# First head's operands moved inside SBUF; second batch's transposes, rotation sums and the bias matmuls placed in the first heads

## What is computed

```
xn = layernorm(x)
# branch A: causal attention, 16 heads of 8 dims, rotary positions
q, k, v = split(xn @ qkv_w.T + qkv_b);  q = rope(q);  k = rope(k)
A = softmax(causal(q @ k.T / sqrt(8))) @ v;  A = A @ out_w.T + out_b
# branch B: six nodes, each an attention of 8 heads of 16 dims over earlier nodes
for c in range(6):
    q = ew[c,0] * (nodes[in_q] @ We[eq] + be[eq]);  k, v likewise
    nodes[c] = act_w[c] * mha(q, k, v, Wq[c], Wk[c], Wv[c], Wo[c]) + q
B = layernorm(nodes[5]) * ln_g + ln_b
return x + A + B
```

## Time and profile before

| | us |
|---|---|
| median of 3 runs (lowest, highest) | 1428.02 (1425.81, 1428.82) |
| profiled execution, device time | 1432.52 |
| profiled execution, span | 1430.7 |
| TensorE busy in the span | 1388.9 (97%) |
| VectorE busy | 1256.0 (88%) |
| ScalarE busy | 1137.6 (80%) |
| GpSimd busy | 447.0 (31%) |
| mean granted TensorE clock, as a share of full speed | 0.986 |

### The profile page before, as it was taken

One profiled execution on the slowest core, in us unless ns is written; L12 is line 12 of the kernel. 1 busy time (PEld: TensorE's weight loads), 2 busy tenths in 40 slices (PEclk: granted clock), 3 DMA queues, 4 the chain that ended last, 5 costly groups with the idle time before them and its releaser, 6 DMA issues.

```text
span 1430.7 us, 60748 instructions
## 1 busy us (share of the span) xinstructions
PE 1388.9 (97%) x26482; PEld 931.6 (65%) x26482; DVE 1256.0 (88%) x1557; ACT 1137.6 (80%) x2127; POOL 447.0 (31%) x932
## 2 busy tenths in 40 slices
PE   6899999999999999999999999999999999999996
PEld 5467777656667566676676665766667666667662
DVE  8788999898989889899898898998989989989784
ACT  3378888688878878888788788887888878878793
POOL 5331114334322332233323332234223432330110
PEclk9899999999999999999999999999999999999997
DMA  8131112344232332333323223333233332321212
GB/s 251 36 126 50 59 51 95 118 130 140 71 122 83 122 106 69 100 105 101 107 80 125 99 76 100 106 114 107 75 100 106 97 109 78 127 97 56 64 40 64
DMA packets 115940, 138.22 MB, mean 97 GB/s; under 512 B 14954, under 2 KB 90347, under 8 KB 115547
## 3 DMA queue, kind: packets, MB, share of 16 engines
q1 hardware_dynamic: 115675, 134.33, 29.0%
HBM read 64.90 MB, written 62.26 MB: 89 GB/s over the span
## 4 chain that ended last, share of the span: by engine, by line
PE 84%; DMA 5%; SPq 4%; DVE 3%; ACT 2%; POOL 2%; issue 1%; ACTq 0%; POOLq 0%; DVEq 0%
PE s L992 51%; PE cps L1087 24%; PE misc L992 8%; DMA qs<-mrows 3%; SPq L419 1%; ACT probs L761 1%; DMA dram_raw_b<-csb 1%; DVE neg_max L942 1%; PE misc L987 1%; SPq L387 1%; SPq L456 1%; DMA ks<-dram_qk_a 0%; DMA ks<-dram_qk_b 0%; POOL parts L585 0%; POOL xtok L644 0%
## 5 line engine op out<-in xcount | busy, mean ns | idle before, releaser
L761 ACT ACTIVATE probs<-s 128x512 f32<-128x512 f32 x1792 | 1059.2, 599 | 227.7 <-PE s L992 166.0
L942 DVE TENSOR_REDUCE neg_max<-s 128x1 f32<-128x1024 f32 x768 | 936.2, 1222 | 71.2 <-PE s L992 16.4
L992 PE MATMUL s<-qs,ks 99*32 99x512 bf16 (+2 forms) x7680 | 808.4, 371 | 8.6 <-DMA qs<-mrows 6.7
L992 PE MATMUL s<-ks,qs 96*32 96x512 bf16 (+2 forms) x7680 | 606.7, 370 | 6.3 <-DMA ks<-dram_qk_a 4.1
L1087 PE MATMUL cps<-probs,vs 128*32 128x256 f32 (+1 forms) x7552 | 590.8, 368 | 0.3 <-ACT probs L761 0.3
L992 PEld LDWEIGHTS s<-qs,ks 99*32 99x32 bf16 x7680 | 235.6, 94 | 245.2 <-ACT probs L761 101.4
L1087 PEld LDWEIGHTS cps<-probs,vs 128*32 128x32 f32 x7552 | 314.4, 110 | 77.5 <-issue 17.1
L992 PEld LDWEIGHTS s<-ks,qs 96*32 96x32 bf16 x7680 | 290.4, 97 | 90.5 <-issue 24.7
L617 POOL TENSOR_TENSOR mparts<-neg_max,zeros 128x8 bf16<-128x8 f32 x128 | 25.8, 201 | 788.7 <-DVE neg_max L942 657.1
L938 DVE CUSTOM_DVE_ANT_0 s<-s,mask_q 128x1024 f32<-128x1024 f32 (+7 forms) x256 | 188.2, 786 | 27.5 <-PE s L992 17.8
L683 POOL TENSOR_TENSOR parts<-full,zeros 128x512 bf16<-128x512 f32 x48 | 61.5, 1282 | 52.8 <-DVE full L918 52.8
(11 more groups left out here) (128 smaller groups left out, 603.2 us busy)
## 6 DMA issues: line engine op xcount, KB each, us to landing
dram_qk_b<-parts SPq DMA_DIRECT2D x48, 384.0 KB, 3.3
qs<-dram_qk_b SPq DMA_DIRECT2D x96, 192.0 KB
ks<-dram_qk_b SPq DMA_DIRECT2D x96, 192.0 KB
dram_qk_b<-parts SPq DMA_DIRECT2D x48, 256.0 KB, 3.2
dram_raw_b<-csb SPq DMA_DIRECT2D x95, 128.0 KB, 4.4
dram_qk_b<-parts SPq DMA_DIRECT2D x48, 128.0 KB, 3.2
vsrc<-srcT SPq DMA_DIRECT2D x12, 512.0 KB, 3.2
ctx_b<-dram_raw_b SPq DMA_DIRECT2D x44, 128.0 KB
```

The lines of the kernel that those rows point to most:

```text
L761: nc.scalar.activation(buf[:, lo:hi], s2[bank][:, 0:hi - lo], ACT.Exp, scale=scale).then_inc(exp_done, 1)
L942: last = ve.tensor_reduce(peak, scores, AX.X, ALU.max, negate=True)
L992: last = te.matmul(dst[c0:c0 + STRIP, :], lhsT[:, c0:c0 + STRIP], rhs, start=start, stop=stop, tile_position=(0, c0))
```

## The change

Seven edits, all around the set-up and phase A0:

1. SP writes only chunks n = 0 and 1 to DRAM at first. Head 0's rows of chunks 2 and 3 (the second 512 tokens of q and k) go from `parts` in SBUF straight into `qs0` and `ks0` (`first_head`, 12 DMAs of 8 rows x 1 KB); the first 512 tokens of head 0 are still read back from DRAM (2 DMAs of 48 rows). The writes of chunks 2 and 3 and the load of head 1 follow. TensorE waits for `first_in` as well before head 0.
2. POOL fills the rows of ones of `ks` before the layer norm, not after it, and DVE's clearing leaves them out.
3. DVE normalises the first batch only; POOL does the second one, and its 8 transposes go into A0, 4 after turn (0, 3) and 4 after (1, 0), each copied out by ACT (`tr`).
4. The 18 one-column bias matmuls go into head 0, 6 after each of turns 0, 1 and 2 (`b0`). Biases 1 to 3 move to (1, 3), (2, 0) and (2, 3). Product 5 moves to (1, 1).
5. In set-up, products 2 to 4 go to the banks `s2_0`, `s2_1`, `cps`; DVE makes the last two low parts instead of POOL.
6. In A0, POOL adds cosine and sine terms of the second batch (four sums, in heads 1 to 4) instead of DVE, ahead of its `rest` and `low_part` of the chunk before. POOL's addition to x moves from head 0 to head 6.
7. The load of head 8 is issued in head 7 of A0 without a wait for the second batch's writes; that wait stands at the end of AL's first round.

```diff
-START_AT = {(0, 0): ("bias", 1), (0, 1): ("bias", 2), (0, 2): ("bias", 3),
-            (0, 4): ("rot", 8), (1, 2): ("rot", 9), (1, 4): ("rot", 10), (2, 2): ("rot", 11),
+START_AT = {(0, 0): ("b0", 0), (0, 1): ("b0", 1), (0, 2): ("b0", 2), (0, 3): ("tr", 2),
+            (0, 4): ("rot", 8), (1, 0): ("tr", 3), (1, 1): ("prod", 5), (1, 3): ("bias", 1), (2, 0): ("bias", 2), (2, 3): ("bias", 3), (1, 2): ("rot", 9), (1, 4): ("rot", 10), (2, 2): ("rot", 11),
             (2, 4): ("rot", 12), (3, 2): ("rot", 13), (3, 4): ("rot", 14), (4, 2): ("rot", 15),
             (4, 4): ("va", 2), (5, 2): ("va", 3)}
...
+        product_bank = [s1[0], s1[0][:, CH:S], s2[0], s2[1], cps, misc]
...
+            def first_head(n, part):
+
+                w, op = n // 2, n % 2
+                lo, hi, step = (Q_ROWS, K_ROWS)[op][part]
+                sp.wait_ge((rope_hi, rope_mid, a_low)[part], n + 1)
+                for r in range(lo, hi, step):
+                    sp.dma_start((qs, ks)[op][0][r * DA:(r + 1) * DA, w * CH:(w + 1) * CH], parts[n][0:DA, part, :]
+                                 ).then_inc(first_in, 16)
+
+            for n in range(NCH):
                 write_a(n, [0])
                 if n:
                     write_a(n - 1, [2])
                 write_a(n, [1])
-            write_a(2 * NCH - 1, [2])
+            sp.wait_ge(dve_const, 3 * RING)
+            first_head(2, 0)
+            write_a(1, [2])
+            first_head(2, 1)
+            first_head(3, 0)
+            first_head(2, 2)
+            for n in range(NCH):
+                sp.wait_ge(a_written[n], 3 * 16)
+                sp.dma_start((qs, ks)[n][0][0:6 * DA, 0:CH], qk_dram["A"][n, :, 0:DA, 0:CH]).then_inc(qk_in[0], 16)
+            first_head(3, 1)
+            first_head(3, 2)
+            for n in (2, 3):
+                write_a(n)
             for s in a_written:
                 sp.wait_ge(s, 3 * 16)
...
-            load_unit("A0", 0, 0, 0)
...
-                    if k == UP - 1 and kind not in ("A0", "BE", "T"):
+                    if (kind, r, k) == ("AL", 0, UP - 1):
+                        for s in a_written:
+                            sp.wait_ge(s, 2 * 3 * 16)
+                    if k == UP - 1 and kind not in ("BE", "T"):
                         load_unit(kind, r, UP, b)
...
-                    if kind == "A0" and k == UP - 1:
-                        for s in a_written:
-                            sp.wait_ge(s, 2 * 3 * 16)
...
-                    if k == UP - 1 and kind == "A0":
-                        load_unit(kind, r, UP, b)
...
+            for s in range(RING):
+                pool.wait_ge(pool_const, 6 + s)
+                pl.memset(ks[s][MROW:128, :], 1.0).then_inc(pool_const, 1)
+            pool.wait_ge(pool_const, 6 + RING)
+            pl.memset(ones_row[:, :], 1.0).then_inc(pool_const, 1)
+            pl.memset(zeros[:, :], 0.0).then_inc(pool_const, 1)
...
-                low_part(n - 1)
-            low_part(2 * NCH - 1)
+                if n < 2 * NCH - 1:
+                    low_part(n - 1)
+            for t in range(TB, TT):
+                pl.tensor_scalar(xn[:, t * D:(t + 1) * D], xtok[:, t * D:(t + 1) * D], mv[:, 2 * t:2 * t + 1],
+                                 rstd[:, t:t + 1], ALU.subtract, ALU.mult).then_inc(xn_late, 1)
...
-                    if kind == "A0" and k == 0:
+                    if kind == "A0" and 1 <= k < 1 + 2 * NCH:
+
+                        n = 2 * NCH + k - 1
+                        pool.wait_ge(rot_done, 2 * n + 2)
+                        pool.wait_ge(a_low, n - STAGES + 1)
+                        pl.tensor_tensor(full[n % STAGES][:, :], rope[0][:, :], rope[1][:, :], ALU.add
+                                         ).then_inc(rope_full, 1)
+                    if kind == "A0" and k == 6:
...
             for n in range(2 * NCH):
                 high_part(n)
-                if n == 0:
-                    transposed(2)
-                    transposed(3)
+                if n == 2:
+                    act.wait_ge(wb_in, 16 * 11)
+                    products(0)
+                if n == 3:
+                    values_a(0)
                 middle_part(n)
-            act.wait_ge(wb_in, 16 * 11)
-            products(0)
             products(1)
-            for g in range(TB // 4):
-                values_a(g)
-            for n in range(2, NODES):
+            values_a(1)
+            for n in range(2, NODES - 1):
                 products(n)
...
-                if what == "va":
+                if what == "tr":
+                    act.wait_ge(xt_ps, w + 1)
+                    nc.scalar.copy(srcT[:, w * CH:(w + 1) * CH], misc[:, :]).then_inc(xt_sb, 1)
+                elif what == "prod":
+                    products(w)
...
-                for ring in (qs[s][:, :], ks[s][:, :], vs[s][:, :, :]):
+                for ring in (qs[s][:, :], ks[s][0:MROW, :], vs[s][:, :, :]):
...
-            for t in range(TT):
-                if t % TB == 0:
-                    dve.wait_ge(ln_pow, t // TB + 1)
+            dve.wait_ge(ln_pow, 1)
+            for t in range(TB):
                 ve.tensor_scalar(xn[:, t * D:(t + 1) * D], xtok[:, t * D:(t + 1) * D], mv[:, 2 * t:2 * t + 1],
                                  rstd[:, t:t + 1], ALU.subtract, ALU.mult).then_inc(xn_ready, 1)
...
-                    ve.tensor_tensor(full[n % STAGES][:, :], rope[0][:, :], rope[1][:, :], ALU.add
-                                     ).then_inc(rope_full, 1)
+                    if n < 2 * NCH:
+                        ve.tensor_tensor(full[n % STAGES][:, :], rope[0][:, :], rope[1][:, :], ALU.add
+                                         ).then_inc(rope_full, 1)
...
+            for n in (2 * NCH - 2, 2 * NCH - 1):
+                dve.wait_ge(rope_mid, n + 1)
+                dve.wait_ge(a_low, n)
+                ve.tensor_tensor(parts[n % STAGES][:, 2, :], full[n % STAGES][:, :], parts[n % STAGES][:, 1, :],
+                                 ALU.subtract).then_inc(a_low, 1)
...
-                        if what == "bias":
-                            biases(g)
+                        if what == "bias" or (what, g) == ("b0", 2):
+                            biases(g * (what == "bias"))
...
+            def transposes(g, bank):
+
+                for t in range(4 * g, 4 * g + 4):
+                    if t < TB:
+                        pe.wait_ge(xn_ready, t + 1)
+                    else:
+                        pe.wait_ge(xn_late, t - TB + 1)
+                    last = te.transpose(bank[:, t % 4 * 128:(t % 4 + 1) * 128], xn[:, t * D:(t + 1) * D], ident[:, :])
+                last.then_inc(xt_ps, 1)
...
                 rotate(m, (s2[0], s2[1], cps, misc)[m % 4])
-                if m == 3:
-                    transposes(1)
                 if m == 5:
                     pe.wait_ge(wb_in, 16 * 11)
                     products(0)
@@ -1040,18 +1075,24 @@
                     products(1)
             pe.wait_ge(wa_in, 16 * 6)
             for g in range(TB // 4):
-                pe.wait_ge(xt_sb, 3 + g)
                 values_a(g, half[2 + g])
+            for n in range(2, 5):
+                pe.wait_ge(rot_done, n + 3)
+                products(n)
+
...
-            biases(0)
-            for n in range(2, NODES):
-                products(n)
-            pe.wait_ge(comp_sb, 3 * NODES)
+            pe.wait_ge(comp_sb, 3 * 2)
+            pe.wait_ge(va_sb, TB // 4)
             pe.wait_ge(pool_const, N_CONST)
...
-                if what in ("bias", "rot", "va"):
-                    return {"bias": bias_used, "rot": rot_done, "va": va_sb}[what], w + 1
+                if what in ("bias", "rot", "va", "tr"):
+                    return {"bias": bias_used, "rot": rot_done, "va": va_sb, "tr": xt_sb}[what], w + 1
+                if what == "b0":
+                    return bias_used, w // 2
+                if what == "prod":
+                    return comp_sb, 3 * (w + 1)
...
                             if i == 0:
                                 pe.wait_ge(qk_in[k % RING], 32 * (2 * ph + k // RING + 1))
+                                if (kind, k) == ("A0", 0):
+                                    pe.wait_ge(first_in, 16 * 12)
```

More of the change, by code:

```diff
@@ L396, in write_a @@
                             [(rope_hi, n + 1), (rope_mid, n + 1), (a_low, n + 1)], only)
-            for n in range(2 * NCH):
+            def first_head(n, part):
[6 more added lines that the diff above has]
+            for n in range(NCH):
                 write_a(n, [0])
@@ L996, in _ @@
             pe.wait_ge(pool_const, 4)
-            def transposes(batch):
-                for t in range(batch * TB, (batch + 1) * TB):
-                    pe.wait_ge(xn_ready, t + 1)
-                    last = te.transpose(half[t // 4][:, t % 4 * 128:(t % 4 + 1) * 128], xn[:, t * D:(t + 1) * D],
-                                        ident[:, :])
-                    if t % 4 == 3:
-                        last.then_inc(xt_ps, 1)
```

(15 more changed lines are left out.)

33 lines of the change are left out of this document (15 added, 18 removed).

## The result

The changed kernel takes 1435.33 us, the median of 5 runs (1434.93 to 1437.83), against 1428.02 for the kernel before. The ratio is 1.0056, with a 95% interval of 1.0043 to 1.0070: slower, by 7.3 us. The forecast had the sign (slower, 0.49) and +3.2 us; the measured loss is more than twice that. Only the "worse" rival (+7.4) had its size.

The account below looks back on a forecast made before the run. From head 0 on TensorE's own stream was taken as the bound, at half clock in head 0. Terms -2.6 + 4.9 + 2.5 + 0.8 + 0.9 - 3.3 = +3.2 on 1428.0 gave 1431.2 us, range 1424.5 to 1436.0.

Parts of the forecast that it names:

- "worse" rival: Copies cost 0.8, head 0 starts at 38.6, half clock through head 1: +7.4 us, 1435.4; chance 0.17.
- term 1: Start of head 0: SP's copies begin at 24.4 at 0.63 each, start at 36.2 instead of 38.8, -2.6 us.
- Term 2: Head 0: three bias groups and four transposes come in, biases 1 to 3 leave; +4.9 us (+2.0 to +5.5).
- Term 3: Head 1: wait for POOL's parts goes; transposes, product 5, ACT waits and bias 1 come in; +2.5 us.
- term 4: Head 2: biases 2 and 3 come in at the full clock, +0.8 us (+0.5 to +1.3).
- term 6: Head 7 to head 8: earlier load removes the wait and half clock behind it, -3.3 us (-2.2 to -3.6).
- term 5: Heads 2 to 4: POOL's sum delays ACT's middle cast, 0.3 a head, three heads: +0.9 us (0 to +3).
- clock that stays up: TensorE returns to full clock by head 0's second group and stays there: -3.5 us, 1424.5; chance 0.15.
- cheap queue: SP's copies of 8 rows cost 0.34 to 0.4, head 0 starts at 33.0: sum 0.0; chance 0.18.
- an expensive queue and a cold head 1: The "worse" rival in full: copies at 0.8, half clock through head 1, +7.4 us; chance 0.17.

## Why the prediction was wrong, point by point

Each of the six terms has the sign that was forecast, and TensorE's stream at the half clock is what the edit ran into in head 0. The sum was wrong by size. By the table above it missed 1.3 us in term 1, 1.6 in terms 2 to 4 up to m2, and 0.5 in term 6, less 0.3 in term 5. Two steps failed in their mechanism: "Biases 2 and 3 come in at the full clock" (term 4), and "I start the copies at 24.4" (term 1).

**Term 1, the start of head 0: -1.3, not -2.6.** The copies began at 25.58. Ahead of them in SP's queue stood the write of the first chunk's low part, which POOL finished at 24.63; SP waited 2.4 us for it, and issued this write and the next until 25.46. The cast that I took for the limit was done at 24.26, and I had called the low parts no limit. From the first copy the queue then took 10.3 us, where 9.4 was forecast; a copy's price of 0.63 was nearly right (8.1 us for twelve). Landing was quicker than the 3.0 taken: 1.79 for the last one. Another 0.3 is the base: 38.80 was the latest start of the three profiles before.

**Term 2, head 0: +5.7, not +4.9.** It went from 10.0 (10.11, 9.30 and 10.63 in the three profiles) to 15.7. The three groups cost 8.16 (7.9 forecast), the transposes and the wait for ACT 1.3 (1.2). So biases 1 to 3 gave back 3.8, not 4.2, and that is no fixed number: bias 1 took 2.62 and 2.72 in the first and third profile of the kernel before, and in the second

```profile
38.88 1.81 PE L987 MATMUL misc<-vbias,comp 128*128 128x1 f32 x12
```

That TensorE would run head 0 at 0.50 was right, and the "clock that stays up" is refuted. The "cheap queue" is too: no copy went out in under 0.62.

**Term 3, head 1: +2.1, not +2.5.** It took 8.03, 9.43 and 9.47 before, at a granted clock of 0.74, 0.50 and 0.50, and 11.06 and 11.17 after, at 0.81 in both. So the clock of this head was not lower than before; what came in cost its own time.

**Term 4, head 2: +2.0, not +0.8.** The part up to m2 took 2.6 in all three profiles before, at a clock of 1.00. After, it took 3.50 at 0.80 and 4.73 at 0.58, +1.5 in the mean where half of the term was +0.4. The half clock had come behind bias 1, at the end of head 1, and reached into head 2. Scores of head 2 that take 0.61 at the full clock, in the second profile of the changed kernel:

```profile
64.48 1.07 PE L1029 MATMUL s<-ks,qs 96*32 96x512 bf16 x8
```

From m2 to m3 it is +0.5, nearly as forecast (0.4).

**Term 5: +0.6, not +0.9.** The mechanism is the one forecast. In head 3, POOL's sum, its subtraction and ACT's middle cast:

```profile
80.37 1.28 POOL L667 TENSOR_TENSOR full<-rope 128x512 f32<-128x512 f32 x1 [3.86 <-DVE rope L866]
81.61 1.16 POOL L617 TENSOR_TENSOR full<-full,parts 128x512 f32<-128x512 f32 x1
```

```profile
82.80 0.62 ACT L738 CAST parts<-full 128x512 bf16<-128x512 f32 x1 [1.55 <-POOL full L617]
```

The cast is 8.7 us into its head, where it was 7.0, 1.7 later. It costs 0.28 in each of two heads, not 0.3 in three.

**Term 6: -2.8 in the mean, not -3.3.** The wait was read rightly and is gone in both profiles of the changed kernel. The half clock behind it was read from one execution and taken for the rule; it follows the wait in two of three. Taken against the second profile alone, the gain is only 1.6. The same fact put the other terms on a base that was itself one draw of several.

The rival that came nearest in time, "an expensive queue and a cold head 1", had another mechanism: its copies at 0.8 and a start of 38.6 didn't happen. Nor did its second half, the half clock through head 1: the clock there was 0.81. That its time came out is luck. What remains between +6.3 by the marks and +7.3 by the medians is within the interval, and no run here settles it.

## What to carry to other kernels

Before work is moved out of a stage in which its engine waits, ask what it costs there: the bias matmuls lay in idle time and came to stand in TensorE's own stream, and putting them back gave the whole loss of the change back. A matmul of one column has no fixed price in a dense stream, since the half clock can come with it, for its neighbours too; keep such matmuls together where the engine idles. And where a term rests on the clock or on a wait's length, take several profiles of the kernel before, and sum by marks inside the program; a stage whose length is the same to 0.01 us in all of them can be booked to that precision, one that varies by 2 us can't.

## What the runs showed of the hardware

- One-column float32 matmuls in the middle of heads at the full clock were followed by a half clock from 96.1 to 106.3 us, and cost 10.3 us for 18 of them instead of the 4.5 of their own time, a wait of 1.26 ahead of them included. They ran at 1.50 for a group of 6 ahead of that, and at 2.72 in it. In the set-up of the kernel before, the clock fell at about 29.2 in the middle of 18 such matmuls, with TensorE busy throughout since 22.
- Full-width products of 128x512 took 11.05 us for ten, from a clock that was at half (it had fallen at about 30.9, among the bias matmuls ahead of them). The clock was at full from 37.6 to 47.9 and then at half again, though head 0 had begun at the full clock at 44.15.
- The same wait of TensorE, 1.6 to 1.8 us, was followed by the half clock in two of three executions of the same kernel, and by none in the third; it costs about 1.8 us (m6 to m9 23.16 and 22.94, against 21.17).
- Copies inside SBUF of 8 rows of 1 KB went out at 0.62 to 0.71 us each from SP, and the last landed 1.79 after its issue. On ACT's queue the first of three took 1.23, with ACT's own work going on beside it; the other two took 1.31 together, the same price, while ACT's own work stood still for 1.45 us.
